# Attention's order on TensorE: where the products for the maxima and the turned outputs stand among scores and weighted values

## The reference

```
qkv = (x @ w_qkv).reshape(Bx, Tx, 3, H, HD)
scores = jnp.einsum('bhqd,bhkd->bhqk', q, k) * SCALE
scores = jnp.where(causal[None, None], scores, -jnp.inf)
geo_bias = q_proj[..., :, None] * k_proj[..., None, :]
scores = scores + head_scales[None, :, None, None] * geo_bias
attn = jax.nn.softmax(scores, axis=-1)
out = jnp.einsum('bhqk,bhkd->bhqd', attn, v)
out = out @ w_out
x = x + layernorm(out)          # then the experts: top 2 of 7 and one shared, SwiGLU
```

## Time and profile before

| | |
|---|---|
| profiled execution, its own time | 487.31 us |
| its span | 485.5 us |
| median of the three runs | 486.38 us |
| busy: PE, DVE, ACT, POOL | 416.2, 325.7, 244.5, 133.8 us |
| attention's groups 0 to 6, each about | 27.6 us |
| group 7 and what follows it up to the second phase | 251 to 288 us |
| experts (PE without a gap) | 350 to 457 us |

### The profile page before, as it was taken

One profiled execution on the slowest core, in us unless ns is written; L12 is line 12 of the kernel. 1 busy time (PEld: TensorE's weight loads), 2 busy tenths in 40 slices (PEclk: granted clock), 3 DMA queues, 4 the chain that ended last, 5 costly groups with the idle time before them and its releaser, 6 DMA issues. The chain is left out here.

```text
span 485.5 us, 10662 instructions
## 1 busy us (share of the span) xinstructions
PE 416.2 (86%) x3980; PEld 255.0 (53%) x3980; DVE 325.7 (67%) x823; ACT 244.5 (50%) x416; POOL 133.8 (28%) x220
## 2 busy tenths in 40 slices
PE   1869899999999999999989878897999999999500
PEld 0533433435243433435244364655699999999500
DVE  5899978797988888797963936499433333333277
ACT  1531167776777677686776707653233233233240
POOL 8200000100111110100110013334667766763332
PEclk9985589999999999999998959999999999999955
DMA  7554750303021020000000017100577687877152
GB/s 218 198 180 142 244 160 20 90 2 88 3 63 28 11 81 2 2 2 4 1 3 3 0 53 208 44 2 0 169 216 248 209 253 247 238 221 239 43 161 86
DMA packets 46694, 50.77 MB, mean 105 GB/s; under 512 B 5363, under 2 KB 34420, under 8 KB 46644
## 3 DMA queue, kind: packets, MB, share of 16 engines
q1 hardware_dynamic: 43632, 44.77, 30.1%
q0 software_dynamic: 2432, 4.99, 3.6%
q10 hardware_dynamic: 580, 0.33, 0.3%
HBM read 36.90 MB, written 12.98 MB: 103 GB/s over the span
## 5 line engine op out<-in xcount | busy, mean ns | idle before, releaser
L640 ACT ACTIVATE probs<-banks 128x1024 f32<-128x1024 f32 (+1 forms) x192 | 145.3, 810 | 59.1 <-PE banks L495 48.0
L786 DVE TENSOR_REDUCE mx_part<-banks 128x1 f32<-128x512 f32 (+2 forms) x224 | 130.2, 646 | 15.9 <-PE banks L476 7.5
L470 PE MATMUL banks<-k_st,q_st 64*128 64x512 bf16 (+3 forms) x384 | 115.7, 354 | 8.0 <-DVE parts L754 4.2
L488 PE MATMUL banks<-q_st,k_st 64*128 64x512 bf16 (+3 forms) x384 | 97.5, 333 | 6.2 <-ACT probs L640 5.9
L507 PE MATMUL banks<-probs,v_pad 128*32 128x512 f32 (+3 forms) x768 | 83.3, 506 | 0.0
L1525 DVE TENSOR_TENSOR hidden<-banks,gate 128x512 f32<-128x512 f32 x38 | 26.3, 692 | 66.2 <-PE banks L1192 66.2
L488 PEld LDWEIGHTS banks<-q_st,k_st 64*128 64x128 bf16 x384 | 31.1, 95 | 60.9 <-ACT probs L640 49.0
L786 DVE TENSOR_REDUCE mx<-banks 128x1 f32<-128x512 f32 (+3 forms) x96 | 51.9, 596 | 16.5 <-PE banks L476 15.2
L470 PEld LDWEIGHTS banks<-k_st,q_st 64*128 64x128 bf16 x384 | 34.4, 95 | 36.3 <-DVE mx_part L786 27.7
L474 PE MATMUL banks<-mask_qk,ident_half 64*128 64x128 bf16 x256 | 52.6, 231 | 0.0
L493 PE MATMUL banks<-mask_kq,ident_half 64*128 64x128 bf16 x256 | 49.3, 221 | 0.0
(11 more groups left out here) (199 smaller groups left out, 572.2 us busy)
## 6 DMA issues: line engine op xcount, KB each, us to landing
w_g<-in_w_gate SPq DMA_DIRECT2D x38, 256.0 KB
w_u<-in_w_up SPq DMA_DIRECT2D x38, 256.0 KB
q_st<-q_rows SPq DMA_DIRECT2D x32, 128.0 KB, 2.9
k_st<-k_rows SPq DMA_DIRECT2D x32, 128.0 KB, 2.9
w_d<-in_w_down SPq DMA_DIRECT2D x8, 256.0 KB, 5.1
back<-results SPq DMA_DIRECT2D x8, 256.0 KB, 4.7
q_rows<-parts SPq DMA_DIRECT2D x4, 384.0 KB, 3.0
k_rows<-parts SPq DMA_DIRECT2D x4, 384.0 KB, 3.5
```

Source lines behind the costliest of these rows:

```text
L470: last = nc.tensor.matmul(dst[:, at:at + width], q_st[r][rows, c, p, (i % CH) * P:(i % CH + 1) * P], k_st[r][rows, kc, p, 0:width], start= ...
L488: last = nc.tensor.matmul(dst[a][:, 0:width], k_st[r][rows, j // CH, p, (j % CH) * P:(j % CH + 1) * P], q_st[r][rows, c, p, first:BANK], s ...
L640: nc.scalar.activation(probs[unit % PROBS][:, 2 * p:2 * p + 2, first:BANK], slot_pair[k % 2].rearrange("p (a t) -> p a t", a=2)[:, :, 0:BA ...
L786: nc.vector.tensor_reduce(dst, taken[:, :, 0:width], AX.X, ALU.max, negate=True).then_inc(max_taken, 1)
```

## The change

In units with four wide products PE's order was score, product, score, product and so on, with the weighted values behind the fourth product. Now the fourth product follows the weighted values. In narrow units all four products now come first, then the four scores, then the weighted values. In group 7 (no products) only the places of the turned outputs change. The outputs are turned at x = 4 and x = 7 in place of x = 1 and x = 6 (`OUT_X`), with their places in the slots, ACT's `take_outputs` and DVE's `invert_sums` (now ahead of x = 6 and x = 9). POOL splits the next group's maxima before it normalises `(n - 1, 1)`. `first_turn_attn` and `first_project` stay at x = 2 and x = 4 of group 7; `invert_sums(6, 1)` stays ahead of the copies in DVE's stream. The number and the shapes of all instructions are the same.

```diff
+OUT_X = (7, 4)
@@ slot_list
-            if x == 1 and n > 0:
+            if x == OUT_X[1] and n > 0:
                 slots.append(("out", n - 1, 1))
-            if x == 6:
+            if x == OUT_X[0]:
                 slots.append(("out", n, 0))
@@ GpSimd
                 split_rows(n, 1, steps + 6 * n + 3)
+                if n + 1 < GROUPS:
+                    split_rows(n + 1, 0, steps + 6 * n + 6)
                 if n > 0:
                     normalise(n - 1, 1)
-                if n + 1 < GROUPS:
-                    split_rows(n + 1, 0, steps + 6 * n + 6)
                 normalise(n, 0)
@@ TensorE
-
+                    ahead = n + 1 < GROUPS
+                    spread = ahead and not MAX_NARROW[x]
+                    if ahead and MAX_NARROW[x]:
+                        for m, (p, a) in enumerate(((0, 1), (0, 0), (1, 1), (1, 0))):
+                            maxima(n + 1, x, p, a, m)
                     for p in range(PAIRS_G):
                         dst = free_slot(("score", n, x, p))
                         score(n, x, p, 0, dst)
-                        if n + 1 < GROUPS:
+                        if spread:
                             maxima(n + 1, x, p, 1, 2 * p)
                         score(n, x, p, 1, dst).then_inc(slot_filled, 1)
-                        if n + 1 < GROUPS:
-                            maxima(n + 1, x, p, 0, 2 * p + 1)
+                        if spread and p == 0:
+                            maxima(n + 1, x, 0, 0, 1)
                     if x > 0:
                         weighted_values(n, x - 1)
                     elif n > 0:
                         weighted_values(n - 1, UNITS - 1)
+                    if spread:
+                        maxima(n + 1, x, 1, 0, 3)
                     if x == 0:
                         turn_maxima(n, 1)
-                    if x == 1 and n > 0:
+                    if x == OUT_X[1] and n > 0:
                         turn_outputs(n - 1, 1)
-                    if x == 6:
+                    if x == OUT_X[0]:
                         turn_outputs(n, 0)
@@ ScalarE takes the outputs at OUT_X too; VectorE
-                    if x == 3 and n > 1:
+                    if x == OUT_X[1] + 2 and n > 1:
                         invert_sums(n - 2, 1)
-                    if x == 8 and n > 0:
+                    if x == OUT_X[0] + 2 and n > 0:
                         invert_sums(n - 1, 0)
```

## The result

The changed kernel took 490.5 us in the median of 20 runs, the kernel before 486.59 in 20. The ratio is 1.0068 (95% interval 1.0049 to 1.0087): 3.3 us slower, 2.4 to 4.2. One run of each kernel, of 808.15 and 766.23 us, fell in a slow state and counts in neither the ratio nor its interval; without them the medians are 489.93 and 486.50. The forecast was 489.0 with 485.5 to 491.8, and +2.6 us.

What follows compares the result with a forecast made beforehand. No engine is full; a loop through three engines bounds each group. Groups 1 to 6 +0.4, group 0 +0.5, group 7 +1.7, sum +2.6 us on 486.38, gave 489.0, range 485.5 to 491.8.

Steps and rivals of the forecast that it cites:

- the prediction's chances: Whole kernel: slower (above 488.8 us) 0.47, same 0.43, faster 0.10, split from the forecast and its rivals.
- The cycle: Wide units: the loop through three banks, now carried by the third product, takes 2.71 us where it binds, against 2.49.
- The pairs of units: Middle group: x = 4, 5 +0.34; 6, 7 +0.04; 8, 9 +0.29; 10, 11 −0.03; 0, 1 −0.49; 2, 3 −0.09; sum +0.06 us.
- The loss of 8 × 0.22 a group: Wide units: parting the fourth product from its score would lose one 0.22 us step each; not taken as a new loss.
- Narrow units: x = 2, 3, 10, 11: PE bounds them, so products first gain nothing inside; 2.89 us against 2.92 for x = 10, 11.
- The wait: Group 7: copies wait behind the reciprocal of outputs turned at x = 4, so the projection ends 1.7 us later.
- PE's two waits: Group 7, from 261 to 263.7: the new stall leaves PE about 0.7 and 1.4 us idle.
- The sign given for the layer norm: Changed profile, group 7: BATCH_NORM_STATS2 starts 14.7 us after the group's start in place of 13.0.
- the cold tail: Rival, end of attention: projection at the lower clock adds up to 2.05 us; +3.5 to +4.7, about 490.5; chance 0.2.
- the forecast's own range: Whole kernel: 487.8 to 490.2 us around the forecast of 489.0; chance 0.45.
- group 0: First group: +0.5 us, from +0.3 in units 6 to 9 and about 0.2 for unit 1's fourth product at half clock.
- A wait I had called unneeded: Middle groups: POOL's split no longer stands behind a wait, and its result is used at x = 5; costs nothing.

Runs made afterwards that it cites:

- e2: Against the kernel before: outputs turned at x = 4 and 7, products for the maxima in the old order; 487.05 us, ratio 1.0003.
- e3: Against the kernel before: new order of the products for the maxima, outputs turned at x = 1 and 6 as before; 489.64 us, ratio 1.0054.
- e4: Against the kernel before: only the narrow units begin with their four products; 485.48 us, ratio 0.9964.
- e6: Against the kernel before: narrow units begin with four products, outputs turned at x = 4 and 7 in groups 0 to 6 only; 484.26 us, ratio 0.9947.
- e8: Against the changed kernel: matmuls of 512 columns that nobody reads put where PE waits in group 7; 488.87 us, ratio 1.0039 to the kernel before.
- e1: Against the changed kernel: DVE's reciprocal of outputs (6, 1) moved behind the two copies; 487.81 us, ratio 1.0017 to the kernel before.
- e5: Against e2: the reciprocal of outputs (6, 1) moved behind the two copies; 484.6 us, ratio 0.9967 to the kernel before.
- e9: Against e6: matmuls that nobody reads put where PE waits around the end of attention; 482.63 us, ratio 0.9928 to the kernel before.
- e7: Against e6: weighted values of units x = 6 and 7 in two halves, fourth product between them; 484.61 us, ratio 0.9950 to the kernel before.

## Why the prediction was right

- **The sign and the size.** +2.6 forecast, +3.3 (2.4 to 4.2) measured; the profiled executions differ by 4.0. In the prediction's chances a hundredth is misplaced: its parts give slower 0.26 + 0.20 = 0.46 and same 0.44, not 0.47 and 0.43; nothing hangs on it.
- **The cycle.** Third product to third product 2.71 forecast, 2.70 seen; period 27.61 and 27.59. The pairs of units came out as walked to 0.04 us, so the small sum is not two large errors that cancel, and the same reading foresaw e2, e3 and e4 to 0.05 us. The loss of 8 × 0.22 a group, which the prediction weighed and turned down, did not come: e3, the products' order alone, loses 0.42.
- **Narrow units** as said in the period: 0.07 us a group alone (e4), nothing beside moved turns (e6). e4 is 1.7 us faster than before all the same, of which the periods explain 0.4; its profiled execution had the upper clock through group 7, before's had not. How much of the rest is clock stays open.
- **Group 7.** The wait was sized 1.7, measured 1.85 (e2 and e8, each against e3) and removed by one moved reciprocal (e1). PE's two waits were foreseen as 0.7 and 1.4, and are 0.61 and 1.27. The sign given for the layer norm, 14.7 us after the group's start, did not come: it was 16.16 (from the first score at 252.35 to 268.51), and 1.19 of the 1.46 between them is the projection, which took 3.24 in place of 2.05.
- **Mis-sized: the clock.** I put no clock into the forecast and gave the cold tail 0.2 beside it. In the profiled executions the clock costs 2.6 us of the last group, 1.3 before, so 1.3 of the 3.15 there. That execution is one of the longer ones (491.33); the median of 489.93 lies in the forecast's own range of 487.8 to 490.2. Whether the stall makes the lower level likelier is not shown: 10 of 19 runs of the changed kernel had a mean clock of 0.926 or less, one of 12 each in e1 and e8, but 6 of 12 in e3, which has no such stall.
- **Mis-sized: group 0.** 0.5 forecast. Counted from first exponential to first exponential it lasts 29.58 against 28.71, so 0.87. Units 1 to 3, the first of them at the lower level of the clock, took 0.40 longer, twice my 0.2, and the rest falls in units 6 to 11.
- **A wait I had called unneeded.** One group (2) lasted 27.93: in x = 4 the score started 0.33 late. SP's transfers of the next operands took 0.95 longer than in other groups (2.21 against 1.26 us for one pair), and the maxima's rows are sent behind them. The shorter x = 0 to 3 took away the slack that had covered this. No run was made to test it, but the traces fit: with unmoved turns such a long transfer cost nothing (before: 2.53, period 27.59; e4: 2.34, 27.49), with moved turns it did (e5: 2.14, period 27.54 in place of 27.25).

## What to carry to other kernels

When an order is changed in a loop through a ring of buffers, write down the cycle (release, matmuls behind it, what stands between, way to the reader) before and after; a long step between a buffer's release and its refill lengthens the cycle, whichever wait it fills (here 0.49 us a group). Then look at the last round, in which the loop's neighbours are different: here the place of one reciprocal in an in-order stream, harmless in the loop, cost more than all the rest. And price a stall of TensorE at its length, and look at the clock granted to the matmuls behind it if they end the path: in one execution here that was 1.3 us more than before.

## What the runs showed of the hardware

- Matmuls of the two halves of the array did not start in the order of the program, so the sentence in the section on the chip, that each engine runs its stream in order, does not hold for the starts of PE's matmuls. Between units 6 and 7 it is: fourth product (half 0), score (half 0), next unit's first product (half 1). The trace has both products at 157.64 and the score at 157.86. A matmul on a busy half did not hold up the next one on the free half.
- In all traces of kernels without added matmuls behind attention the clock was at the lower level for 10 to 14 us from about 276 to 286 us on; with sixteen added matmuls (e9) it was not. That is one profiled execution, and the mean clocks go with it: 0.934 to 0.941 in e9's seven runs, 0.924 to 0.933 in e6's six. So matmuls whose result nobody reads count as activity. That activity lifts the throttle is the Trainium skill's rule ("TensorE: Matmul & The Clock Gate", Part 1); the trace agrees, with 1.00 in e9 and 0.53 in e6 between 280 and 290 us.
- The weighted values of four heads, 32 columns of the array each, run side by side: their eight passes over 512 queries take 1.00 us (156.64 to 157.64), where three added matmuls of 512 columns in e8 take 0.67 one after the other (260.94 to 261.61), so eight would take about 1.8, an estimate from these. Over 256 queries they take 0.57 (e7).
